# A graph network's last stage: the last node chunk in two parts, and up to six dense steps beside a gathered row

## The chip, the cores and the metric

One core of one Trainium2 chip runs the kernel. The metric is the device time of one execution in microseconds; 4676.03 us is the median of three runs of the kernel before (4673.82 to 4677.75). In the text PE is TensorE, DVE is VectorE, ACT is ScalarE, POOL is GpSimd and SP is SyncE.

## What is computed

A graph of 6250 nodes (64 features) and 200000 edges, sorted by target node. The first part is a two-layer edge-typed graph attention network with a residual and a layer norm. The second part, on which the change works, is this (`W`, `b` small, `pos`/`neg` the positive and negative part of the cosine):

```python
x  = layernorm(x + L0(x))              # two layers over the edges
Wh = x @ W + b
sim = cosine(Wh[src], Wh[dst])
base = edge_weight * softplus(deg[0] * edge_weight_n2 + deg[1]) * (src != dst)
prop = segment_sum(base * (c0 * relu(sim) - c1 * relu(-sim)) * Wh[dst], src)
out = layernorm(x + scale * (prop + c2 * Wh))
```

## The kernel before

The edges lie in 112 rows of 14 tiles of 128 edges. Because the targets are sorted, the targets of a row fall into a window of 80 nodes. Stages run one after another: a table of messages per node, `fast_path(0)`, a second table, `fast_path(1)` with the first 56 rows of layer 1, and then `last_rows` (L993), the only stage that the change touches. It does three things at once.

**The last 56 rows of layer 1.** For each row GpSimd issues 14 indirect gathers into `lrows` (L1158), which has four row buffers (`RB`), so a row's gather waits until the row four before it is used up. ACT scales the 14 tiles by the edge weights (L1351, in four parts, "wt"), DVE builds a one-hot matrix (L1411, "hot"), PE multiplies the two (L1248, "sum"), and DVE adds the result to the node sums `feat`, a window wide (L1422, "add", which also frees the buffer).

**The chunks of nodes.** Once all rows that reach a chunk of 7 node tiles (896 nodes) are added, the chunk can be finished: 19 steps over PE, DVE, ACT and SP (`STEPS`) turn the sums back, add residuals, apply the layer norm (`layer`, `centre`, `layer2`; L1428 to L1446), form `Wh` (`bias`, L1471), store it to memory, normalise it (`unit`, L1480), turn it in two halves (`HALF`), copy strips of it (ACT, L1378, "win") and load strips of `Wh` (SP, "load"). `needs` is the number of rows that must be added first: 0, 0, 0, 9, 25, 41 and 56 for the seven chunks.

**The dense part.** `fast_path` has stored for each of 56 groups of edges a dense matrix of edge weights, 128 targets by all 6272 nodes. A dense step, a "unit" (b, p), takes one pair of groups p (28 of them) and one block b of 448 nodes (14 of them), so there are 392. PE makes cosines (L1219), ACT takes their positive part (L1342), DVE blends (L1395) and multiplies with the loaded block of the matrix (`weigh`, L1147), and PE adds the product (L1238) into a PSUM bank. In a row DVE does every multiplication; after the rows GpSimd does every second one. Cosines have two buffers; the product runs three units behind. Consecutive units of one block are a visit. At its end DVE copies or adds the bank to `out_t` (`kept`, L1397, here called a block sum; L1403 is the add); the last visit of each block is copied by ACT instead (L1339) and goes into the output. A chunk's units can only run when the chunk is finished: chunk c opens its own two blocks for all pairs so far, and for older blocks the pairs that it adds (`READY`: 3, 7, 11, 15, 19, 23, 28 pairs). Before the rows end one bank is used, then two alternate.

**The order** is written out by a planner (L1022) that all engines follow. Between the parts of a row it calls `some`, which puts up to two chunk steps and one unit in the plan: four times around the scaling, and `OWN - 4` times between a row's sum and its add.

```python
OWN = 5
for c in range(NCH):
    first_of.append(len(units))
    for b in range(2 * c + 2):
        ps = range(before[c] if b < 2 * c else 0, READY[c])
...
if todo_u < first_of[done // len(STEPS)]:
    plan.append(("unit", todo_u))
```

A unit is planned only when its chunk is complete, so a chunk whose rows are not yet there leaves the calls empty. The plan has 256 units in the rows (4 and 2 in rows 0 and 1, five in most; none in rows 25 and 41, one in rows 26 and 42, four in rows 24 and 40) and 136 behind them. The last visits of blocks 2c and 2c+1 are followed by output chunk c: PE turns it (L1309, L1311), DVE adds and normalises (`result`, L1458 to L1469), SP stores. There are seven.

Of the kernel before, what the change touches and what calls it, by code (L numbers as in the profile page):

```python
# [14 lines left out]
P = 128  # L15
F = 64
# [44 lines left out]
READY = [4 * (c + 1) - 1 for c in range(NCH - 1)] + [PAIRS]  # L61
# [12 lines left out]
def build(nc, A, out):  # L74
    ctx = ExitStack()
    with ctx:
# [916 lines left out]
        def last_rows():  # L993

            CB, NA, LAG = 4, 4, 3
            OWN = 5
# [12 lines left out]
            first_visit = len(visits) - 2 * NCH  # L1009
# [58 lines left out]
            with ExitStack() as s4, scope() as s12, nc.Block() as block:  # L1068
# [19 lines left out]
                stage_u = both[:, :].rearrange("p (c a f) -> p c a f", c=CH, a=2)  # L1088
# [22 lines left out]
                s_whg = [ls(f"whg{c}") for c in range(NCH)]  # L1111
# [3 lines left out]
                HALF = ((0, 4), (4, CH - 4))  # L1115
# [4 lines left out]
                def tiles(c):  # L1120
                    return slice(c * CH, (c + 1) * CH)

# [41 lines left out]
                def _(sp):  # L1164
# [10 lines left out]
                    for event in plan:  # L1175
# [5 lines left out]
                        elif event[0] == "fin":  # L1181
                            c, step = event[1:]
                            if step == "store":
# [5 lines left out]
                                sp.dma_start(wh_rows.ap()[c * CH * P:(c + 1) * CH * P, :].rearrange("(i p) f -> p i f", p=P), skip[:, tiles(c), :]).then_inc(s_tab, 16)  # L1189
# [12 lines left out]
                    sp.wait_ge(s_whg[NCH - 1], 16 * len(groups_of(NCH - 1)))  # L1202
# [4 lines left out]
                def _(pe):  # L1207
                    def cosines(u):
                        b, p = units[u]
                        for c in range(NCH):  # L1210
# [11 lines left out]
                    def product(u):  # L1222
# [3 lines left out]
                        for c in range(NCH):  # L1226
# [24 lines left out]
                    def turn(c, half, src, width, s):  # L1251
                        lo, n = HALF[half]
# [4 lines left out]
                    def x_tile(c, j):  # L1257
                        return x_sb[:, c * CH + j, :]
# [4 lines left out]
                    for event in plan:  # L1263
# [8 lines left out]
                        elif event[0] == "fin":  # L1272
                            c, step = event[1:]
                            if step == "back":
                                if needs[c]:
                                    pe.wait_ge(s_add, needs[c])
                                if c:
                                    pe.wait_ge(s_uk, 2 * c)
                                for j in range(CH):
                                    last = pe.transpose(ps_h[:, j * F:(j + 1) * F], feat[:, (c * CH + j) * P:(c * CH + j + 1) * P], ident[0:F, 0:F])  # L1280
# [4 lines left out]
                            elif step == "xt1":  # L1285
                                pe.wait_ge(s_xk, 2 * c + 1)
                                turn(c, 1, x_tile, F, s_xt)
                            elif step == "wh":
                                pe.wait_ge(s_xk, 2 * c + 2)
                                for j in range(CH):  # L1290
# [5 lines left out]
                            elif step == "ut1":  # L1296
                                pe.wait_ge(s_uk, 2 * c + 1)
                                turn(c, 1, u_tile, P, s_ut)
                        elif event[0] == "out" and event[2] == "turn":
                            c = event[1]  # L1300
                            emptied(pe, first_visit + 2 * c + 1)
                            if c < NCH - 1:
                                pe.wait_ge(s_o_free, first_visit)
                            pe.wait_ge(s_uk, 2 * NCH)
                            if c:
                                pe.wait_ge(s_ovar, c)
                            for j in range(CH):
                                if c < NCH - 1:
# [9 lines left out]
                def _(act):  # L1318
# [3 lines left out]
                    def unit_kept(c, half):  # L1322
                        lo, n = HALF[half]
                        at = (c * CH + lo) * P
# [4 lines left out]
                    for event in plan:  # L1329
# [24 lines left out]
                        elif event[0] == "fin":  # L1354
                            c, step = event[1:]
                            if step == "std":
                                act.wait_ge(s_var, c + 1)
                                act.activation(mom[:, 2, tiles(c)], mom[:, 1, tiles(c)], ACT.Sqrt).then_inc(s_std, 1)
                            elif step in ("xk0", "xk1"):
                                half = int(step[2])  # L1360
                                lo, n = HALF[half]
                                act.wait_ge(s_xt, 2 * c + half + 1)
                                act.activation(xt[:, lo * P:(lo + n) * P], ps_h[0:F, 0:n * P], ACT.Copy).then_inc(s_xk, 1)
                            elif step == "nrm":
                                act.wait_ge(s_sq, c + 1)
                                act.activation(mom[:, 3, tiles(c)], mom[:, 0, tiles(c)], ACT.Sqrt).then_inc(s_nrm, 1)
                            elif step in ("uk0", "uk1"):
                                half = int(step[2])
                                act.wait_ge(s_ut, 2 * c + half + 1)
# [3 lines left out]
                            elif step == "win":  # L1373
                                act.wait_ge(s_uk, 2 * c + 2)
# [11 lines left out]
                def _(dve):  # L1386
# [10 lines left out]
                    def kept(k):  # L1397
                        b, lo, hi = visits[k]
                        part = out_t[:, b * SB:(b + 1) * SB]
                        dve.wait_ge(s_prod, hi + 1)  # L1400
                        if again[k]:
                            dve.wait_ge(s_o_free, again[k][-1] + 1)
                            dve.tensor_tensor(part, part, bank(k)[:, 0:SB], ALU.add).then_inc(s_o_free, 1)  # L1403
                        else:
                            dve.tensor_copy(part, bank(k)[:, 0:SB]).then_inc(s_o_free, 1)
# [8 lines left out]
                    def add_sums(r):  # L1414
# [6 lines left out]
                        part = feat[:, bass.ds(window, WIN)]  # L1421
                        dve.tensor_tensor(part, part, ps_sum[0:F, 0:WIN], ALU.add).then_inc(s_add, 1)  # L1422

                    def spread(ap, n):
                        return ap.rearrange("p (i o) -> p i o", o=1).to_broadcast([P, CH, n])

                    def centre(i, s_done):
                        link(dve.tensor_reduce(mom[:, 0, i], t1[:, :, :], AX.X, ALU.add))  # L1428
                        link(dve.tensor_scalar(mom[:, 0, i], mom[:, 0, i], 1.0 / F, None, ALU.mult))
                        link(dve.tensor_tensor(t1[:, :, :], t1[:, :, :], spread(mom[:, 0, i], F), ALU.subtract))  # L1430
                        link(dve.tensor_tensor(t2[:, :, :], t1[:, :, :], t1[:, :, :], ALU.mult))
                        link(dve.tensor_reduce(mom[:, 1, i], t2[:, :, :], AX.X, ALU.add))
                        dve.tensor_scalar(mom[:, 1, i], mom[:, 1, i], 1.0 / F, EPS_LN, ALU.mult, ALU.add).then_inc(s_done, 1)

                    def layer(c):
                        i = tiles(c)
                        dve.wait_ge(s_back, c + 1)
                        link(dve.tensor_tensor(t1[:, :, :], ps_h[:, 0:CH * F].rearrange("p (c f) -> p c f", f=F), skip[:, i, :], ALU.add))
                        link(dve.tensor_tensor(t1[:, :, :], t1[:, :, :], x_sb[:, i, :], ALU.add))
                        centre(i, s_var)  # L1440

                    def layer2(c):
                        i = tiles(c)
                        dve.wait_ge(s_std, c + 1)
                        link(dve.reciprocal(mom[:, 3, i], mom[:, 2, i]))
                        dve.tensor_tensor(x_sb[:, i, :], t1[:, :, :], spread(mom[:, 3, i], F), ALU.mult).then_inc(s_xn, 1)  # L1446
# [9 lines left out]
                    def result(c):  # L1456
# [4 lines left out]
                        centre(i, s_ovar)  # L1461

                    def result2(c):
# [5 lines left out]
                        dve.tensor_tensor(ready[c % 2], t1[:, :, :], spread(mom[:, 1, i], F), ALU.mult).then_inc(s_ready, 1)  # L1469

                    def bias(c):  # L1471
                        i = tiles(c)
                        dve.wait_ge(s_wh, c + 1)
                        dve.tensor_tensor(skip[:, i, :], ps_h[:, 0:CH * F].rearrange("p (c f) -> p c f", f=F),
                                          b2[:, :].rearrange("p (o f) -> p o f", o=1).to_broadcast([P, CH, F]), ALU.add).then_inc(s_skip, 1)
                        dve.wait_ge(s_skip, c + 1)
                        link(dve.tensor_tensor(t2[:, :, :], skip[:, i, :], skip[:, i, :], ALU.mult))
                        dve.tensor_reduce(mom[:, 0, i], t2[:, :, :], AX.X, ALU.add).then_inc(s_sq, 1)

                    def unit(c):  # L1480
                        i = tiles(c)
# [285 lines left out]
```

## Time and profile before

| | us |
|---|---|
| runs, median of 3 | 4676.03 (4673.82 to 4677.75) |
| the profiled execution, its own time | 4682.8 |
| its span in the profile | 4679.8 |
| PE busy | 3153.3 (67%) |
| DVE busy | 3124.3 (67%) |
| ACT busy | 1572.7 (34%) |
| GpSimd busy | 3240.7 (69%) |

The profile is one execution, a hardware trace of every instruction. The page groups it; the windows view cuts it into stretches with each engine's busy time, the granted clock of TensorE (1.00 is 2.4 GHz, 0.50 is 1.2 GHz) and the DMA share; the timeline lists instructions in order, with the idle time before each on its engine and what ended it in square brackets. A wait for several things is put down to the one that came last. `last_rows` begins at about 3297 us and ends at 4671 us.

### The profile page before, as it was taken

To read this page: it belongs to the slowest core of one execution; us is meant where nothing else is said; L and a number is where in the kernel's file an instruction comes from. 1 tells how busy PE (TensorE), PEld (TensorE's weight loads), DVE (VectorE), ACT (ScalarE), POOL (GpSimd) and SP (SyncE) were. 2 spreads that over 40 slices of the span, in tenths; PEclk is the share of its full clock that TensorE was granted. 3 is DMA by queue.
4 is the path that set the end of the run, shared out by engine and by line. 5 is a ranking of instruction groups with operands and counts; after the bars stand their busy time and mean duration, and the time that the engine had idled before them with its cause. 6 is when DMAs were issued, how large, how long until landed. Compare 5 with 4: busy or idle time off the path is not lost. (4 is left out here: it accounts for less than half of the span.)

```text
span 4679.8 us, 63684 instructions
## 1 busy us (share of the span) xinstructions
PE 3153.3 (67%) x16225; PEld 1888.5 (40%) x16225; DVE 3124.3 (67%) x5180; ACT 1572.7 (34%) x3260; POOL 3240.7 (69%) x3224
## 2 busy tenths in 40 slices
PE   4676777677777677676555656555476767677888
PEld 3344554445455444454344434444222222322232
DVE  6776777667777777774655555554477767677787
ACT  3422323232322322233421221221344545444434
POOL 0577777777777777774477777776666777776556
PEclk7888888888888888887777877787588989889999
DMA  3333323233333333332322222222355545555566
GB/s 63 122 93 91 97 90 101 83 96 93 97 94 90 98 91 95 92 97 80 111 72 67 77 71 68 76 72 66 110 155 144 165 125 165 137 152 155 169 176 193
DMA packets 355301, 502.07 MB, mean 107 GB/s; under 512 B 93127, under 2 KB 214984, under 8 KB 354809
## 3 DMA queue, kind: packets, MB, share of 16 engines
q1 hardware_dynamic: 251689, 394.52, 26.0%
q0 software_dynamic: 100352, 102.96, 10.7%
q8 instruction: 124, 2.03, 0.2%
q14 instruction: 240, 1.97, 0.1%
q10 hardware_dynamic: 2896, 0.59, 0.1%
HBM read 290.63 MB, written 207.16 MB: 106 GB/s over the span
## 5 line engine op out<-in xcount | busy, mean ns | idle before, releaser
L835 POOL DMA_INDIRECT frows<-messages,fidx x2352 | 2290.5, 974 | 828.5 <-issue 669.1
L915 PE MATMUL fps_b<-hot_key,hot_lo 128*128 128x343 f32 x3136 | 1237.8, 501 | 415.3 <-PEq L71 408.4
L974 DVE TENSOR_TENSOR strip<-strip,fps_b 128x343 f32 x1568 | 787.7, 502 | 552.9 <-DVEq L71 540.8
L850 ACT ACTIVATE turned<-fps_t 128x512 f32<-128x512 f32 (+1 forms) x754 | 431.9, 573 | 1755.6 <-ACTq L71 1749.2
L905 PE MATMUL fps_sum<-hot,frows 128*64 128x80 f32 x4704 | 555.1, 303 | 600.1 <-PEq L71 600.1
L1158 POOL DMA_INDIRECT lrows<-messages,lidx x784 | 744.9, 950 | 295.4 <-issue 223.2
L915 PEld LDWEIGHTS fps_b<-hot_key,hot_lo 128*128 128x128 f32 x3136 | 540.7, 206 | 742.4 <-issue 695.9
L905 PEld LDWEIGHTS fps_sum<-hot,frows 128*64 128x64 f32 x4704 | 526.3, 196 | 688.8 <-issue 688.8
L944 DVE TENSOR_SCALAR hot_key<-iota_f,edge 128x343 f32<-128x343 f32 x1574 | 751.5, 478 | 0.2
L1342 ACT ACTIVATE pos<-l_c,coeff 128x896 f32<-128x896 f32 x392 | 394.7, 1007 | 580.7 <-PE l_c L1219 579.8
L1219 PE MATMUL l_c<-unit_t,unit_g 64*128 64x448 f32 x1568 | 434.7, 632 | 132.7 <-DVE acc L1147 70.6
L899 PE MATMUL fps_t<-ident,strip 128*128 128x128 f32 x2842 | 474.4, 291 | 33.2 <-PEq L71 33.2
L899 PEld LDWEIGHTS fps_t<-ident,strip 128*128 128x128 f32 x2842 | 379.6, 151 | 234.0 <-issue 107.1
L841 ACT ACTIVATE strip<-zcol 128x512 f32<-128x512 f32 (+2 forms) x758 | 470.9, 621 | 0.0
L1395 DVE SCALAR_TENSOR_TENSOR l_c<-l_c,coeff,pos 128x896 f32<-128x896 f32 x256 | 295.1, 1153 | 253.4 <-ACT pos L1342 252.5
L988 DVE TENSOR_TENSOR frows<-frows,edge 128x896 f32<-128x896 f32 x168 | 182.6, 1087 | 291.0 <-DMA frows<-messages,fidx 288.5
L938 DVE TENSOR_TENSOR hot_lo<-fps_iota,edge 128x896 f32<-128x896 f32 x226 | 246.0, 1089 | 140.6 <-issue 139.6
L1238 PE MATMUL l_o<-acc,wh_g 128*64 128x448 f32 x1008 | 266.8, 610 | 71.4 <-DVE sums_t L1403 53.8
L1219 PEld LDWEIGHTS l_c<-unit_t,unit_g 64*128 64x128 f32 x1568 | 128.0, 198 | 391.6 <-DVE acc L1147 126.6
L938 DVE TENSOR_TENSOR hot<-fps_iota,edge 128x1120 f32<-128x1120 f32 x168 | 220.7, 1314 | 0.0
L1147 DVE TENSOR_TENSOR acc<-l_c,edge 128x896 f32<-128x896 f32 x192 | 209.5, 1091 | 6.6
L1351 ACT ACTIVATE lrows<-lrows,edge 128x64 f32<-128x64 f32 x784 | 208.6, 336 | 15.1 <-DMA lrows<-messages,lidx 15.0
(191 smaller groups left out, 1936.5 us busy)
## 6 DMA issues: line engine op xcount, KB each, us to landing
adj<-turned SPq DMA_DIRECT2D x696, 256.0 KB
edge<-adj SPq DMA_DIRECT2D x294, 448.0 KB
adj_x<-adj SPq DMA_DIRECT2D x98, 448.0 KB
frows<-messages,fidx POOLq DMA_INDIRECT x2352, 2.4
messages<-msg SPq DMA_DIRECT2D x14, 1120.0 KB, 4.6
lrows<-messages,lidx POOLq DMA_INDIRECT x784
adj<-turned SPq DMA_DIRECT2D x58, 64.0 KB
wh_g<-wh_rows SPq DMA_DIRECT2D x56, 32.0 KB, 1.8
```

Source lines behind the costliest of these rows:

```text
L835: pool.indirect_dma_start(rows[:, q, k, :], None, tab_l[l].ap(), bass.IndirectOffsetOnAxis(ap=idx[:, q, k:k + 1], axis=0)).then_inc(s_got[ ...
L841: return act.activation(part, zcol[:, 0:1].rearrange("p (a b) -> p a b", a=1).to_broadcast([P, n, STRIP]), ACT.Copy)
L850: act.activation(turned[j][:, 0:(b - a) * P], ps_t[j][:, 0:(b - a) * P], ACT.Copy).then_inc(s_t_free, 1)
L899: last = pe.transpose(ps_t[side(k, piece)][:, n * P:(n + 1) * P], strip[k][:, hi, :], ident[:, :])
L905: last = pe.matmul(ps_sum[0:F, 0:WIN], rows[:, u % RB, k, :], hot[:, u % 2, k, :], start=(k == 0), stop=(k == JT - 1))
L915: pe.matmul(ps_b[n % KB][:, 0:NT * TWIN], hot_lo[:, s % 2, k, :], hot_key[:, n % KB, :], start=True, stop=True).then_inc(s_b, 1)
L938: return dve.tensor_tensor(out_ap, ps_iota[:, 0:width].rearrange("p (o c) -> p o c", o=1).to_broadcast([P, n, width]), per_edge(array, at, ...
L944: dve.tensor_scalar(hot_key[:, n % KB, :], iota_f[:, :], edge[:, A_KEY, bass.ds(at, 1)], edge[:, A_BASE, bass.ds(at, 1)], ALU.is_equal, AL ...
L974: dve.tensor_tensor(part, part, ps_b[n % KB][:, 0:NT * TWIN].rearrange("p (h w) -> p h w", w=TWIN), ALU.add).then_inc(v, 1)
L1158: pool.indirect_dma_start(rows[:, q, k, :], None, tab_l[1].ap(), bass.IndirectOffsetOnAxis(ap=idx[:, q, k:k + 1], axis=0)).then_inc(s_got[ ...
L1219: last = pe.matmul(ps_c[u % 2][:, h, 0:SB], unit_g[h * F:(h + 1) * F, p, :], unit_t[h * F:(h + 1) * F, b * SB:(b + 1) * SB], start=True, s ...
L1342: act.activation(pos[:, u % 2, :, :], ps_c[u % 2][:, :, 0:SB], ACT.Relu, scale=coeff[:, 4:5]).then_inc(s_pos, 1)
```

## The change

The chunks of the dense part no longer have one size. Their bounds are a table of tiles, `BOUNDS`, in which the last chunk of 7 tiles is divided into one of 4 (512 nodes) and one of 3 (384). `SIZE`, `BLOCKS` (448-node blocks that are complete), `READY`, `needs` and the semaphore counts come from it: `READY` is 3, 7, 11, 15, 19, 23, 25, 28, and `needs` is 0, 0, 0, 9, 25, 41, 51, 56. A chunk of at most four tiles has one part instead of two halves and 15 steps. `OWN` is 6, so two units may stand between a row's sum and its add. Block 12 is complete with the new seventh chunk and block 13 with the last, and the first 12 blocks are visited once more: 69 visits instead of 56, 392 units as before. The final turn of the last output chunk now also reads `out_t`, whose last block is cleared beforehand. The operations of a chunk work on its own number of tiles.

```diff
-            OWN = 5
+            OWN = 6
+            BOUNDS = (0, 7, 14, 21, 28, 35, 42, 46, 49)
+            NC = len(BOUNDS) - 1
+            SIZE = [hi - lo for lo, hi in zip(BOUNDS, BOUNDS[1:])]
+            BLOCKS = [P * hi // SB for hi in BOUNDS[1:]]
+            READY = [(P * hi - 352) // 224 + 1 for hi in BOUNDS[1:-1]] + [PAIRS]
+            HALVES = [((0, 4), (4, n - 4)) if n > 4 else ((0, n),) for n in SIZE]
+            HB = [sum(len(k) for k in HALVES[:c]) for c in range(NC + 1)]
...
-            for c in range(NCH):
+            upto = [0] * NSB
+            for c in range(NC):
                 first_of.append(len(units))
-                for b in range(2 * c + 2):
-                    ps = range(before[c] if b < 2 * c else 0, READY[c])
+                for b in range(BLOCKS[c]):
+                    if BLOCKS[c] % 2 and c < NC - 2 and b < BLOCKS[c - 1]:
+                        continue
+                    ps = range(upto[b], READY[c])
+                    upto[b] = READY[c]
                     visits.append((b, len(units), len(units) + len(ps) - 1))
                     units += [(b, p) for p in ps]
...
-            needs = [max(0, 16 * (c + 1) + 1 - first_row) if c < NCH - 1 else n_rows for c in range(NCH)]
+            needs = [max(0, -(-P * BOUNDS[c + 1] // SLOPE_ROW) + 1 - first_row) if c < NC - 1 else n_rows for c in range(NC)]
...
-            chain = [(c, step) for c in range(NCH) for step in STEPS]
+            chain = [(c, step) for c in range(NC) for step in STEPS if SIZE[c] > 4 or step not in ("xt1", "xk1", "ut1", "uk1")]
+            chunks_done = [sum(1 for k in range(n) if chain[k][1] == "load") for n in range(len(chain) + 1)]
...
-                    if todo_u < first_of[done // len(STEPS)]:
+                    if todo_u < first_of[chunks_done[done]]:
...
                             for j in range(CH):
-                                if c < NCH - 1:
-                                    pe.matmul(ps_h[:, j * F:(j + 1) * F], out_t[:, (c * CH + j) * P:(c * CH + j + 1) * P], eye2[:, :], start=True, stop=False)
+                                pe.matmul(ps_h[:, j * F:(j + 1) * F], out_t[:, (c * CH + j) * P:(c * CH + j + 1) * P], eye2[:, :], start=True, stop=False)
                                 at = c % 4 * CH * P + j * P
-                                last = pe.matmul(ps_h[:, j * F:(j + 1) * F], rest_t[:, at:at + P], eye2[:, :], start=(c == NCH - 1), stop=True)
+                                last = pe.matmul(ps_h[:, j * F:(j + 1) * F], rest_t[:, at:at + P], eye2[:, :], start=False, stop=True)
...
-                    def centre(i, s_done):
-                        link(dve.tensor_reduce(mom[:, 0, i], t1[:, :, :], AX.X, ALU.add))
+                    def centre(i, m, s_done):
+                        a, b = t1[:, 0:m, :], t2[:, 0:m, :]
+                        link(dve.tensor_reduce(mom[:, 0, i], a, AX.X, ALU.add))
...
                     def layer2(c):
-                        i = tiles(c)
+                        i, m = part(c), SIZE[c]
+                        if c == NC - 1:
+                            dve.memset(out_t[:, (NSB - 1) * SB:NSB * SB], 0.0).then_inc(s_zero, 1)
```

## Rows read from the trace of the kernel before

**Rows 1.** The page of the kernel before, its first line.
```profile
span 4679.8 us, 63684 instructions
```
**Rows 2.** Windows of the last stage: stretch, us, busy per engine, clock, DMA share, GB/s.
```profile
3512.70:3568.40 55.70, 38.95 (x179) 16.46 (x179) 33.90 (x44) 23.06 (x58) 32.23 (x33) 0.79 0.42 112
3568.40:3791.80 223.40, 165.01 (x936) 63.23 (x936) 175.34 (x177) 117.11 (x281) 168.01 (x178) 0.96 0.61 168
3791.80:3830.90 39.10, 17.88 (x107) 12.56 (x107) 13.38 (x22) 13.36 (x44) 29.66 (x32) 0.65 0.22 51
3830.90:4044.50 213.60, 157.78 (x884) 59.94 (x884) 165.85 (x168) 109.64 (x259) 161.49 (x172) 0.96 0.60 167
4044.50:4097.00 52.50, 27.88 (x159) 17.88 (x159) 23.33 (x33) 21.04 (x67) 39.70 (x43) 0.67 0.32 80
4097.00:4324.80 227.80, 163.67 (x876) 61.92 (x876) 165.48 (x167) 108.11 (x253) 157.23 (x167) 0.92 0.58 156
4324.80:4374.70 49.90, 34.79 (x137) 11.71 (x139) 30.97 (x41) 17.31 (x28) 14.30 (x6) 0.76 0.34 94
...
4659.00:4671.30 12.30, 4.70 (x28) 2.17 (x26) 7.97 (x13) 0.75 (x2) 2.86 (x1) 0.82 0.00 0
```
**Rows 3.** The gathers of L1158: durations, GpSimd's idle before them, and who waits.
```profile
L1158 POOL DMA_INDIRECT lrows<-messages,lidx x784: 938/945/1561, 3296.7 to 4303.9; - x196
...
  issue: 223.2, 724
  POOLq L71: 72.2, 60
...
  ACT lrows L1351: 15.0, 4
```
**Rows 4.** Timeline: start, us, instruction. First gathers of rows 14, 41, 55; add of 55.
```profile
3568.55 0.94 POOL L1158 DMA_INDIRECT lrows<-messages,lidx  x1 [11.93 <-POOLq L71]
...
4042.82 0.94 POOL L1158 DMA_INDIRECT lrows<-messages,lidx  x1 [0.30 <-issue]
...
4287.62 0.94 POOL L1158 DMA_INDIRECT lrows<-messages,lidx  x1 [0.30 <-issue]
...
4324.82 0.22 DVE L1422 TENSOR_TENSOR sums_t<-sums_t,l_sum 64x80 f32 x1
```
**Rows 5.** Timeline of DVE, one row of five steps, from add to add.
```profile
3967.90 0.22 DVE L1422 TENSOR_TENSOR sums_t<-sums_t,l_sum 64x80 f32 x1
...
3980.89 1.16 DVE L1395 SCALAR_TENSOR_TENSOR l_c<-l_c,coeff,pos 128x896 f32<-128x896 f32 x1 [2.70 <-ACT pos L1342]
...
3983.09 0.22 DVE L1422 TENSOR_TENSOR sums_t<-sums_t,l_sum 64x80 f32 x1
```
**Rows 6.** Groups by line and form, 3200 to 4680 us: count, busy us, mean ns, idle before.
```profile
L1395 DVE SCALAR_TENSOR_TENSOR l_c<-l_c,coeff,pos 128x896 f32<-128x896 f32 x256 | 295.1, 1153 | 253.4 <-ACT pos L1342 252.5 <-issue 0.9
...
L1147 DVE TENSOR_TENSOR con_x<-l_c,adj_x 128x896 f32<-128x896 f32 x64 | 69.8, 1091 | 2.2
...
L1403 DVE TENSOR_TENSOR sums_t<-sums_t,l_o 128x448 f32<-128x448 f32 x30 | 18.2, 608 | 0.0
...
L1430 DVE TENSOR_TENSOR t<-t,mom 128x448 f32<-128x448 f32 x14 | 8.8, 625 | 2.1
```
**Rows 7.** Timeline behind the rows, PE and DVE.
```profile
4353.49 1.12 PE L1254 MATMUL l_h<-ident,both 128*128 128x128 f32 x4 [7.17 <-DVE both L1485]
...
4375.49 1.02 PE L1219 MATMUL l_c<-unit_t,unit_g 64*128 64x448 f32 x4
...
4377.35 1.02 PE L1219 MATMUL l_c<-unit_t,unit_g 64*128 64x448 f32 x4
...
4418.07 2.49 DVE L1458 SCALAR_TENSOR_TENSOR t<-skip,coeff,x_sb 128x448 f32<-128x448 f32 x1
...
4445.42 2.50 DVE L1458 SCALAR_TENSOR_TENSOR t<-skip,coeff,x_sb 128x448 f32<-128x448 f32 x1
...
4663.76 1.77 PE L1311 MATMUL l_h<-eye,lrows 128*128 128x64 f32 x14 [0.64 <-ACT lrows L1339]
```

More of the change, by code:

```diff
@@ L1110, in last_rows @@
                     ls(n) for n in ("back", "var", "std", "xn", "xt", "xk", "wh", "skip", "sq", "nrm", "u", "ut", "uk", "win"))
-                s_whg = [ls(f"whg{c}") for c in range(NCH)]
+                s_whg = [ls(f"whg{c}") for c in range(NC)]
                 s_oback, s_ovar, s_ostd, s_ready, s_gain = (ls(n) for n in ("oback", "ovar", "ostd", "ready", "gain"))
@@ L1121, in tiles, with part @@
                     return slice(c * CH, (c + 1) * CH)
+                def part(c):
+                    return slice(BOUNDS[c], BOUNDS[c + 1])
                 def weighed(eng, u):
@@ L1209, in cosines @@
                         b, p = units[u]
-                        for c in range(NCH):
+                        for c in range(NC):
                             if u == first_of[c]:
@@ L1225, in product @@
                         _, lo, hi = visits[k]
-                        for c in range(NCH):
+                        for c in range(NC):
                             if u == first_of[c]:
@@ L1277, in _ @@
                                 if c:
-                                    pe.wait_ge(s_uk, 2 * c)
-                                for j in range(CH):
-                                    last = pe.transpose(ps_h[:, j * F:(j + 1) * F], feat[:, (c * CH + j) * P:(c * CH + j + 1) * P], ident[0:F, 0:F])
+                                    pe.wait_ge(s_uk, HB[c])
+                                for j in range(SIZE[c]):
+                                    at = (BOUNDS[c] + j) * P
+                                    last = pe.transpose(ps_h[:, j * F:(j + 1) * F], feat[:, at:at + P], ident[0:F, 0:F])
                                 last.then_inc(s_back, 1)
@@ L1365, in _ @@
                                 act.wait_ge(s_sq, c + 1)
-                                act.activation(mom[:, 3, tiles(c)], mom[:, 0, tiles(c)], ACT.Sqrt).then_inc(s_nrm, 1)
+                                act.activation(mom[:, 3, part(c)], mom[:, 0, part(c)], ACT.Sqrt).then_inc(s_nrm, 1)
                             elif step in ("uk0", "uk1"):
                                 half = int(step[2])
-                                act.wait_ge(s_ut, 2 * c + half + 1)
+                                act.wait_ge(s_ut, HB[c] + half + 1)
                                 if c == 0 and half == 0:
@@ L1402, in kept @@
                             dve.wait_ge(s_o_free, again[k][-1] + 1)
-                            dve.tensor_tensor(part, part, bank(k)[:, 0:SB], ALU.add).then_inc(s_o_free, 1)
+                            dve.tensor_tensor(total, total, bank(k)[:, 0:SB], ALU.add).then_inc(s_o_free, 1)
                         else:
-                            dve.tensor_copy(part, bank(k)[:, 0:SB]).then_inc(s_o_free, 1)
+                            dve.tensor_copy(total, bank(k)[:, 0:SB]).then_inc(s_o_free, 1)
                     def weights(r):
@@ L1420, in add_sums @@
                             dve.wait_ge(s_add, r)
[L1421 to L1425, printed above, removed]
-                    def centre(i, s_done):
-                        link(dve.tensor_reduce(mom[:, 0, i], t1[:, :, :], AX.X, ALU.add))
+                        sums = feat[:, bass.ds(window, WIN)]
@@ new lines, in add_sums, with spread, turned @@
+                        dve.tensor_tensor(sums, sums, ps_sum[0:F, 0:WIN], ALU.add).then_inc(s_add, 1)
+                    def spread(ap, m):
+                        return ap.rearrange("p (i o) -> p i o", o=1).to_broadcast([P, m, F])
+                    def turned(m):
+                        return ps_h[:, 0:m * F].rearrange("p (c f) -> p c f", f=F)
+                    def centre(i, m, s_done):
+                        a, b = t1[:, 0:m, :], t2[:, 0:m, :]
+                        link(dve.tensor_reduce(mom[:, 0, i], a, AX.X, ALU.add))
@@ L1439, in layer @@
-                        link(dve.tensor_tensor(t1[:, :, :], t1[:, :, :], x_sb[:, i, :], ALU.add))
-                        centre(i, s_var)
+                        link(dve.tensor_tensor(t1[:, 0:m, :], turned(m), skip[:, i, :], ALU.add))
+                        link(dve.tensor_tensor(t1[:, 0:m, :], t1[:, 0:m, :], x_sb[:, i, :], ALU.add))
+                        centre(i, m, s_var)
                     def layer2(c):
-                        i = tiles(c)
+                        i, m = part(c), SIZE[c]
```

72 lines of the change are left out of this document (34 added, 38 removed).

## The prediction, made before the changed kernel ran

> **What bounds the kernel now.** The page gives the span [rows 1], and the change touches only the last stage, `last_rows`, so I cut that stage with the windows view [rows 2]. Busy shares decide nothing there (no engine is above 80% in the rows); what matters is who waits for whom. Three regimes show.
>
> Rows 0 to 55 are paced by two loops tied together. GpSimd issues 14 gathers a row: 945 ns plus the issue gap 223.2/724 = 0.31 us [rows 3], and the gathers of rows 41 and 55 start at 4042.82 and 4287.62 [rows 4]: 244.80/14 = **17.49 us a row**. A gather may start only when the row four before it is added, and where that is late GpSimd stands: 72.2 us in all, 32 of them before the stage, 11.93 at row 14 [rows 3, 4]. The other loop is PE, ACT and DVE. A row with five dense steps and no block sum takes 3983.09 - 3967.90 = 15.19 us from one add to the next, 2.70 of them DVE waiting behind PE's row sum [rows 5]. A step costs DVE 1153 + 1091 ns [rows 6], 2.24 us, so a row has 15.19 - 5 x 2.24 = 4.0 us of its own. Rows 11 to 24 (69 steps) took 223.4 us: 14 x 4.0 + 69 x 2.24 = 210.6, and 12.8 left for nine block sums that DVE drains there; rows 27 to 39 leave 16.0 for ten [rows 2]. I take 1.5 us a sum: 0.6 on DVE, and by the code PE's next block waits until its one bank is drained. Five-step rows, 16 us, are faster than the gather, so the gather sets the pace late in the stage.
>
> After row 55 nothing is gathered. Two steps' first matmuls lie 4377.35 - 4375.49 = 1.86 us apart [rows 7], PE without a gap: **PE-bound at 1.855**. Each output chunk adds 27.35 - 10 x 1.855 = 8.8 us [rows 7]. Between them the last chunk's chain: in 49.9 us only 12 steps run [rows 2] (22.3 us worth), **27.6 us lost**.
>
> **The change part by part.** Working both plans out from the code: 392 steps either way. Before, 256 lie in rows and 136 behind them. After, 271 in rows and 121 behind; rows 2 to 19, 27 to 37 and 43 to 55 hold six, but rows 21 to 25 and 39 to 41 hold none, because steps of a chunk wait until its nodes are summed (rows 25, 41, now also 51) and six a row use them up sooner. So the sixth step does not spread the work, it packs it.
>
> *Six a row.* 4.0 + 6 x 2.24 = 17.4 us, with about 0.9 sum a row 18.7: slower than 17.49. The 120 steps before row 25's chunk end at row 20, not 24, saving four row overheads: 3791.8 - 4 x 4.0 = 3775.8 (before, it is compute that paces up to here, GpSimd standing until row 14). Row 19 was added 13.0 before: 3762.8. Gather 23 cannot start sooner, gather 24 at 3780.3, gather 25 at **3797.8**. Before, gather 25 started 16 rows before gather 41: 4042.82 - 279.8 = 3763. The gather is 35 us late and cannot catch up, since it has no slack; five empty rows only let compute wait for it.
>
> *Rows 25 and 26.* ACT scales a row in order, before the chunk's square root, so it waits for the data. From gather start to add takes 4324.82 - 4287.62 = 37.2 [rows 4], less the 15.2 of a row: data 22 us after the start, 3819.8. The two rows with the chunk chain took 39.1 us with one step [rows 2], now three: 43.6, less 5 for the eight short DVE steps that run while ACT waits: row 26 ends at 3858.4. The same sum for rows 41 and 42 of before gives 4042.8 + 22 + 39.1 - 5 = 4098.9; it was 4097.0 [rows 2].
>
> *Rows 27 to 55.* Rows 27 to 37: 11 x 4.0 + 66 x 2.24 + 10 x 1.5 = 206.8, to 4065.2. Gather 41 starts at 3797.8 + 279.8 = 4077.6, row 42 ends at 4077.6 + 22 + 43.6 - 5 = 4138.2. Rows 43 to 55: 13 x 4.0 + 78 x 2.24 + 12 x 1.5 = 244.7, and the new four-tile chain in rows 51 to 53. A seven-tile chain in full rows cost, in rows 9 and 10, 55.7 - 8 - 22.4 - 2 x 1.5 = 22.3 [rows 2]; by tiles alone 12.7. I take 14, nearer the low end, as it also lacks both second halves. On SP it puts one more store, then four table loads, ahead of block loads; those run four ahead. Row 55 is added at 4396.9, against 4324.8: **+72**. By the gather alone it would be 4077.6 + 244.8 + 37.2 = 4359.7: the late rows are compute-bound now.
>
> *The tail.* Fifteen steps fewer: -27.8. The last chain has three tiles, six window copies on ACT instead of ten and 54 steps beside it, not 20, but only two chain steps go between two steps. It stood longest on DVE, 7.17 us at once [rows 7]. A DVE operation has a size-free part: 625 ns at 448 wide and 1091 at 896 [rows 6] give 159 ns, so 192 wide costs 358, which I keep, not 268. Bounds of its loss: 27.6 x 3/7 = 11.8, and 27.6; I take 16.6, **-11**. Thirteen block sums more, 608 ns each [rows 6], come in the tail, where two banks alternate. Two steps take PE 3.71 us and DVE 2 x 1153 + 1091 = 3.4 us, since GpSimd multiplies every other one, so part of each is hidden: from 0 to 13 x 1.5 = 19.5, I take **+3**. The clear of the last block (no wider than a 448-wide operation) hides while the square root is awaited; uncovered it costs 0.6. The last output turn has 28 matmuls, not 14, which took 1.77 [rows 7]: +1.8, on the path. Tail: **-34**.
>
> **Rivals.**
> *A, faster: the extra steps fall into idle time.* For it: DVE is busy under 80% of the row windows, and ACT waits 15.0 us for gathered rows [rows 3], time that is free. If rows with six steps stay under 17.49 us, row 55 stays at 4324.8 and the tail gives 34: **4642**. It decides where a six-step row with its sums is under the gather's time. Against: of the 15.19 us DVE waits 2.70, for PE's row sum, and a sixth step behind that sum waits no less, so it adds its 2.24.
> *B, no change: only the early rows are late.* Gather 25 is 35 us late as worked out, but the last 13 rows keep up with it (block sums or the chain hide): row 55 at 4359.7, +34.9 - 34 = +1: **4677**.
> *C, slower still.* The chain in rows costs the full 22.3, the last chain gains nothing, the sums in the tail cost 19.5: +8 + 11 + 16.5 more: **4750**. For it: DVE's L1458 takes 2.49 us [rows 7] where others of its width take 0.625 [rows 6], with GpSimd multiplying beside it; if the thirteen sums met that, 1.87 us each, it would be 24 instead of 19.5. Against: a sum reads one PSUM bank and one SBUF tile, as L1395 does at 1153 ns, while L1458 reads two SBUF tiles; but the 608 ns were measured while GpSimd only gathered. The Trainium skill (SBUF — State Buffer, "SBUF: two separate sides") says that DVE operations with two SBUF inputs and GpSimd's operations exclude each other from a shared port pair. By that rule the sums are spared; the stretched L1458 agrees with it.
>
> **How the numbers follow.** The summed case 0.64, A 0.12, B 0.16, C 0.08. I trust the lateness of the gather most, since before every row up to 14 the same four-row rule shows as GpSimd standing; I trust the chain costs least. The main case itself spans 4694 to 4734 (chain in rows 12.7 to 22.3, last chain 11.8 to 27.6, sums 0 to 19.5, not all at one end). The range reaches down to B and below, 4668, and up towards C, 4738, leaving A and part of C out. Faster 0.12, same 0.16, slower 0.72.
>
> **What would show it.** Right: gather 25 starts near 3798 and gather 55 near 4322, with GpSimd standing some 35 us more than 72.2 in all before row 25; adds in rows 27 to 37 about 18.7 us apart and in rows 21 to 24 at the gather's pace; row 55 added near 4397; some 312 us from there to the end, against 346. Wrong: six-step rows under 17.5 us, row 55 below 4360, a chain of waits in the tail that names block sums, or a gain in the tail far from 34.

## The result, and the profile after

The changed kernel takes **4710.82 us** (median of 4 runs, 4704.14 to 4720.15) against 4676.89 (4, 4673.82 to 4679.33): ratio 1.0075, 95% interval 1.0063 to 1.0087. The forecast was 4714. The execution profiled took 4720.15 us, 9.3 above the median, with this page in place of [rows 1]:

```profile
span 4718.5 us, 63770 instructions
```

First the three quantities that the prediction tied together: a row with six steps, the gather of row 25, and the end of the rows. Timeline of DVE and GpSimd (start us, duration, instruction, idle before):

```profile
3748.32 0.22 DVE L1433 TENSOR_TENSOR sums_t<-sums_t,l_sum 64x80 f32 x1
3765.70 0.22 DVE L1433 TENSOR_TENSOR sums_t<-sums_t,l_sum 64x80 f32 x1
...
3794.06 0.23 DVE L1433 TENSOR_TENSOR sums_t<-sums_t,l_sum 64x80 f32 x1 [8.81 <-PE l_sum L1260]
3811.39 0.23 DVE L1433 TENSOR_TENSOR sums_t<-sums_t,l_sum 64x80 f32 x1 [15.87 <-PE l_sum L1260]
...
3858.48 0.22 DVE L1433 TENSOR_TENSOR sums_t<-sums_t,l_sum 64x80 f32 x1
```

```profile
3802.41 0.94 POOL L1170 DMA_INDIRECT lrows<-messages,lidx  x1 [0.30 <-issue]
...
4328.54 0.94 POOL L1170 DMA_INDIRECT lrows<-messages,lidx  x1 [0.54 <-issue]
```

The first pair are the adds of rows 18 and 19: 17.38 us apart, six steps and no block sum. Rows 23 and 24 have no steps left, and DVE stands for their sums: there the gather paces. It starts row 25 at 3802.4 and row 55 at 4328.5, 40.9 us behind [rows 4]. What GpSimd waited for in its gathers:

```profile
L1170 POOL DMA_INDIRECT lrows<-messages,lidx x784: 938/944/1819, 3297.4 to 4344.8; - x196
...
  issue: 223.8, 721
  POOLq L70: 112.1, 63
```

The issue gaps are those of [rows 3]; the wait for a free row buffer grew from 72.2 to 112.1 us. Windows cut at the same events as [rows 2] (us, busy per engine, clock, DMA share, GB/s): rows 11 to 24, 25 and 26, 27 to 37, 41 and 42, 43 to 55, then the last chain:

```profile
3593.60:3811.40 217.80, 152.91 (x848) 62.91 (x848) 151.06 (x154) 105.61 (x267) 152.15 (x162) 0.88 0.54 148
3811.40:3858.50 47.10, 20.99 (x119) 12.49 (x119) 17.57 (x27) 16.17 (x49) 35.82 (x38) 0.67 0.26 60
3858.50:4065.90 207.40, 158.32 (x840) 56.92 (x840) 164.93 (x165) 104.14 (x233) 156.80 (x167) 0.95 0.63 173
4091.60:4138.60 47.00, 20.56 (x119) 12.19 (x119) 17.52 (x26) 16.10 (x49) 35.72 (x38) 0.67 0.26 60
4138.60:4398.90 260.30, 196.56 (x1004) 71.94 (x1004) 199.32 (x210) 123.94 (x277) 156.59 (x166) 0.91 0.59 160
4398.90:4430.00 31.10, 23.60 (x91) 7.25 (x91) 21.15 (x37) 11.98 (x19) 11.43 (x4) 0.83 0.44 123
```

Row 55 is added at 4398.94, 74.1 us later than before, and the last instruction stands 310.4 us behind it, where it stood 346.3. In the tail, the timeline of PE and DVE: the longest stall of the last chain, an output's first operation, and the last turn.

```profile
4415.78 0.33 PE L1266 MATMUL l_h<-ident,both 128*128 128x128 f32 x1 [3.53 <-DVE both L1503]
...
4537.38 2.50 DVE L1475 SCALAR_TENSOR_TENSOR t<-skip,coeff,x_sb 128x448 f32<-128x448 f32 x1
...
4557.30 2.50 DVE L1475 SCALAR_TENSOR_TENSOR t<-skip,coeff,x_sb 128x448 f32<-128x448 f32 x1
...
4700.39 0.43 PE L1320 MATMUL l_h<-eye,sums_t 128*128 128x64 f32 x2 [0.64 <-ACT lrows L1350]
```

The stall is 3.53 us for 7.17 [rows 7]. Outputs are 19.93 us apart (the last two pairs 20.4), six steps and 8.8 us, the same surcharge as before. By the count of steps and the times all seemed explained; the experiments showed that it was not.

### The profile page after: what moved, and what is told of

The parts are those of the page before. It is cut to its first block and busy times, and to the rows that moved or that the text cites. A ratio compares the mean times of both kernels' runs of the same rounds, so it can differ in the third digit from the quotient of the medians.

```text
span 4718.5 us, 63770 instructions
## 1 busy us (share of the span) xinstructions
PE 3175.1 (67%) x16239; PEld 1896.0 (40%) x16239; DVE 3140.2 (67%) x5218; ACT 1572.2 (33%) x3262; POOL 3214.7 (68%) x3216
## 5 line engine op out<-in xcount | busy, mean ns | idle before, releaser
L1406 DVE SCALAR_TENSOR_TENSOR l_c<-l_c,coeff,pos 128x896 f32<-128x896 f32 x271 | 312.5, 1153 | 238.0 <-ACT pos L1353 237.9
L1250 PE MATMUL l_o<-acc,wh_g 128*64 128x448 f32 x1096 | 296.5, 622 | 65.3 <-DVE sums_t L1414 48.9
L1159 POOL TENSOR_TENSOR acc<-acc,edge 128x896 f32<-128x896 f32 x60 | 168.7, 2812 | 183.3 <-DVE acc L1406 173.9
L1159 DVE TENSOR_TENSOR acc<-l_c,edge 128x896 f32<-128x896 f32 x204 | 222.7, 1092 | 7.0
```

## The experiments

Every run is given as its median and its ratio to the kernel before, run beside it on the same chip (4676.8 to 4679.6 us in the four groups of runs). The intervals reach 0.1 to 0.14 per cent to either side.

### Split and sixth step apart

**E1**, the changed kernel with `OWN = 5`.
```diff
-            OWN = 6
+            OWN = 5
```

> The changed kernel with OWN = 5: the last chunk divided, five steps a row as before. My theory (the sixth step costs, the split is about neutral): gather 25 starts where it did before (3762), row 55 is added 3 to 8 us later than before because of the four-tile chain in rows 51 to 53 (its 14 us stand against the slack of five-step rows under the gather), and the tail behind it gives 136 steps as before with a chain 11 us cheaper, 2 to 3 us for the block sums and 1.8 for the last turn: 4673 to 4679 us, no change. Rival (the split itself is what costs, through its thirteen sums and its second chain): over 4690.

Measured 4657.46 us (4653.48 to 4661.86), 0.9960 [0.9947, 0.9974]: a gain of 19 us that no theory had. Counted from the stage's first gather, row 55 is added 1.1 us later than before; the whole gain lies in the tail, 324.4 us for 346.3.

**E2**, the kernel before with `OWN = 6`.
```diff
-            OWN = 5
+            OWN = 6
```

> The kernel before with OWN = 6: no split, up to six steps a row. My theory: gathers as late as in the changed kernel (gather 25 near 3802), row 55 added near 4384 (the changed kernel's 4398.9 less its chain of 15 us in the rows), 15 steps fewer behind it at 1.855 us: 59 - 28 = +31, 4704 to 4712 us. Rival (six steps gain by themselves and the split spoils it): below 4677.

Measured 4687.71 us, 1.0018 [1.0008, 1.0028]: dearer, as the theory has the sign, but 16 us below its range.

**E3**, the changed kernel, sixth step up to row 42 only, and **E4**, from row 43 only.
```diff
-                some(OWN - len(PARTS), r)
+                some((6 if r < 43 else 5) - len(PARTS), r)
```

> The changed kernel with six steps only in rows 0 to 42 and five behind. My theory: the late gather is caused here, so gather 25 still starts near 3802 and gather 55 near 4328; rows 43 to 55 then keep up with the gather, row 55 is added near 4368, 258 steps lie in the rows: 4368 + 335 against 4671, +30 us, 4700 to 4712. Rival (the late rows, compute-bound at six, carry the loss): 4680 or less.

Measured 4696.43 us (4689.3 to 4698.97), 1.0037 [1.0023, 1.0050]: 4 us below the theory's range and 16 above the rival's. Row 55 is added at 4374.0 (4368 expected), and the tail is 313.7 instead of 335.
```diff
-                some(OWN - len(PARTS), r)
+                some((6 if r >= 43 else 5) - len(PARTS), r)
```

> The changed kernel with five steps in rows 0 to 42 and six only behind. My theory: gather 25 and row 42 as before (3762, 4097), rows 43 to 55 take 260 us as in the changed kernel, row 55 added near 4357, 269 steps in the rows, tail 315 us: +1, 4673 to 4683 us, so the late six cost nothing and gain nothing. Rival (late rows carry the loss): 4700 or more.

Measured 4677.45 us, 1.0001 [0.9992, 1.0010]. So the early sixth steps carry the cost, the late ones next to none. But E1 and E2 don't add: the split is worth -0.40 per cent with five steps and +0.57 with six.

### The gather's lateness by itself

A fifth row buffer in the last stage lets a gather start when the row five before it is added, not four. `t1` and `t2` move into spare memory to make room, and GpSimd's loop is written out; the steps and their order stay.
```diff
+LRB = 5
...
-                rows = sb("lrows", [P, RB, JT, F], F32, s4)
+                rows = sb("lrows", [P, LRB, JT, F], F32, s4)
-                t1 = sb("t1", [P, CH, F], F32, s4)
-                t2 = sb("t2", [P, CH, F], F32, s4)
+                t1 = spare_a[:, 6 * SB:6 * SB + CH * F].rearrange("p (i f) -> p i f", f=F)
+                t2 = spare_e[:, 6 * SB:6 * SB + CH * F].rearrange("p (i f) -> p i f", f=F)
```
**E5**, in the changed kernel:

> The changed kernel with five row buffers in the last stage instead of four (two small tiles moved into free space, GpSimd's loop written out). My theory (a gather waits for the add four rows before, and that makes it late): with five it waits for the add five rows before, so gather 25 starts one row earlier, near 3784 instead of 3802, row 26 ends near 3841, row 55 near 4381: 17 us less than the changed kernel, 4690 to 4697. Rival (the lateness is the compute of six-step rows alone, the buffers don't matter): as the changed kernel, 4706 to 4714.

Measured 4695.51 us, 1.0035 [1.0021, 1.0049]. **E6**, in the kernel before:

> The kernel before with five row buffers. My theory: GpSimd stands some 9 us instead of 24 after the stage has begun, gathers of rows 15 on start about 15 us earlier, compute stays ahead to row 40 as it was and from there is no longer held by the gather: row 55 added 10 to 14 us earlier, 4662 to 4667. Rival (the late rows are bound by compute already): 4673 to 4680, no change.

Measured 4663.88 us, 0.9974 [0.9965, 0.9983]. Both lie in the theory's range. Counted from the stage's first gather, the gather of row 25 starts 18.0 us earlier in E5 than in the changed kernel and row 55 is added 16.9 earlier; in E6 it is 20.9 and 15.2 against the kernel before. So in both kernels the rows follow the gather's start. It isn't the loop written out that helps: the gathers of 14 rows (41 to 54) take 245.2 us in both runs, 244.8 in the kernel before. But the buffer doesn't undo the change either: with five buffers the change costs 0.61 per cent, with four 0.75, and the difference lies inside the intervals. E5's gathers, with the wait for a row buffer down from 112.1 to 93.1 us:

```profile
L1171 POOL DMA_INDIRECT lrows<-messages,lidx x784: 938/944/1816, 3294.7 to 4322.9; - x196
...
  POOLq L71: 93.1, 60
```

### Why E1, E2 and E3 have shorter tails

From the add of row 55 to the last instruction the traces have, in us, beside what the terms of the prediction make of it:

```
                     tail    by the terms   GpSimd's steps   outputs stand at
before               346.3   (given)        odd              odd steps
changed              310.4   312.3          even             even
E4 six late          314.9   316.0          even             even
E1 split, five       324.4   340.1          odd              even
E2 whole, six        301.6   318.5          even             odd
E3 six early         313.7   336.4          odd              even
```

After the rows GpSimd multiplies every other step, counted from the first one left (`(u - alone) % 2 == 1`). `alone` is 256 before and in E1, 271 in the changed kernel and E2, 258 in E3, 269 in E4. By the plans the outputs (but for the last) come right behind steps 289, 299, ... with the whole chunk and 334, 340, ... with the split one. Where both parities agree the tail is the long one, where they don't it is 16 to 23 us shorter than worked out. (E3 has the most: against E1 another 4.4 us in the steps beside the last chain and 1.9 in the last output, which the parity doesn't account for.) The timeline shows what an output meets. Kernel before, an output's first and last operation on DVE, and GpSimd's products:

```profile
4418.07 2.49 DVE L1458 SCALAR_TENSOR_TENSOR t<-skip,coeff,x_sb 128x448 f32<-128x448 f32 x1
4420.71 0.68 DVE L1460 SCALAR_TENSOR_TENSOR t<-l_h,gain,t 128x448 f32<-128x448 f32 x1
...
4428.68 2.17 DVE L1469 TENSOR_TENSOR both<-t,mom 128x448 f32<-128x448 f32 x1
```

```profile
4417.35 2.73 POOL L1147 TENSOR_TENSOR acc<-acc,edge 128x896 f32<-128x896 f32 x1 [0.97 <-DMA edge<-adj]
4427.50 2.86 POOL L1147 TENSOR_TENSOR con_x<-con_x,adj_x 128x896 f32<-128x896 f32 x1 [7.42 <-DVE con_x L1395]
```

GpSimd's first product ends at 4417.35 + 2.73 = 4420.08 and L1458 at 4420.56, 0.48 later; the second ends at 4430.36 and L1469 at 4430.85, 0.49 later. The next experiments turn the parity and nothing else (where 121 steps are left, GpSimd has 61 products instead of 60).
```diff
-            on_pool = [u for u in range(alone, len(units)) if (u - alone) % 2 == 1]
+            on_pool = [u for u in range(alone, len(units)) if (u - alone) % 2 == 0]
```
**E7**, in the kernel before:

> The whole chunk, five steps a row, but after the rows GpSimd multiplies the other parity of steps: those at an even distance from the first of them instead of those at an odd one. The same work for every engine (68 of 136 products on GpSimd either way). Theory (parity of the outputs): an output part whose first blend (2.50 us) and last product (2.16 us), both with two inputs in SBUF, run beside a GpSimd product costs VectorE 2.1 us more than one that runs clear of it (1.45 and 1.12 us in the kernel split with five steps); seven outputs turn from the first sort to the second, so 346 us after the last row become 331 to 334, and the time 4661 to 4665 us. Rival (the shorter tails of the runs with another number of steps have to do with the split or with where the rows end): nothing changes, 4674 to 4681 us.

Measured 4667.58 us (4661.01 to 4671.63), 0.9977 [0.9967, 0.9986]. It lies between the two ranges, 3 us above the theory's and 6 below the rival's, and its interval leaves out 1. Its tail is 336.2, 10.1 shorter: its outputs come 24.75 us apart (twice 25.4) instead of 27.35, which is 14 us with the last one, but the steps beside the last chain take 4 us longer. The same places in its timeline, DVE, then GpSimd:

```profile
4410.65 1.45 DVE L1458 SCALAR_TENSOR_TENSOR t<-skip,coeff,x_sb 128x448 f32<-128x448 f32 x1
4412.50 0.68 DVE L1460 SCALAR_TENSOR_TENSOR t<-l_h,gain,t 128x448 f32<-128x448 f32 x1 [0.40 <-PE l_h L1311]
...
4420.30 1.12 DVE L1469 TENSOR_TENSOR both<-t,mom 128x448 f32<-128x448 f32 x1
```

```profile
4408.82 2.79 POOL L1147 TENSOR_TENSOR acc<-acc,edge 128x896 f32<-128x896 f32 x1 [0.90 <-DMA edge<-adj]
4418.07 2.87 POOL L1147 TENSOR_TENSOR acc<-acc,edge 128x896 f32<-128x896 f32 x1 [6.45 <-DVE acc L1395]
```

GpSimd's product began earlier against the output here, ends at 4411.61, and L1458 ends at 4412.10, again 0.49 later; L1469 ends at 4421.42, 0.48 behind a product that ends at 4420.94. The instruction isn't slowed in proportion: it ends half a microsecond after GpSimd is done, whenever it began. That holds in every trace: 181 operations of this width with two SBUF inputs began while a product was running, and all ended 0.48 or 0.49 us behind it. The 1346 blends into which PSUM goes (L1395) that began beside one took 1.14 or 1.15 us, as they do alone. The Trainium skill (SBUF — State Buffer, "SBUF: two separate sides") describes this as "an exclusive lock, not a bandwidth split", held for a whole instruction, between a DVE operation with two SBUF inputs and a GpSimd operation; these ends agree with it.

**E8**, the changed kernel turned:

> The changed kernel (split, up to six steps a row) with the other parity of GpSimd's steps after the rows. Theory (parity of the outputs): its outputs take 2.50 and 2.16 us in those two instructions as before's do, and turn to 1.45 and 1.12: 310 us after the last row become 295 to 299, and the time 4694 to 4699 us. Rival (parity is nothing): 4706 to 4715 us.

Measured 4703.72 us, 1.0041 [1.0027, 1.0055]: again between the two ranges, 5 us above the theory's and 2 below the rival's. Both operations went as expected (below), and the tail is 296.1 for 310.4, inside its range. Against the changed kernel's 1.0075 the turn gained 0.34 per cent, 16 us.

```profile
4537.62 1.46 DVE L1475 SCALAR_TENSOR_TENSOR t<-skip,coeff,x_sb 128x448 f32<-128x448 f32 x1
...
4547.28 1.11 DVE L1486 TENSOR_TENSOR both<-t,mom 128x448 f32<-128x448 f32 x1
```

**E9**, the split with five steps (E1), turned:

> The split with five steps a row, with the other parity of GpSimd's steps after the rows. Theory (parity): its outputs here turn the wrong way, to 2.50 and 2.16 us, and its 324 us after the last row become 336 to 340, so 4670 to 4677 us: within 0.2 per cent of the kernel before, as the prediction priced the split by itself. Rival (the split itself gains the 20 us): 4653 to 4662 us as without the turn.

Measured 4680.45 us, 1.0003 [0.9994, 1.0012]: the whole gain of E1 is gone, and some 3 us more than I had put on it. Its tail is 348.8, not 336 to 340, against E1's 324.4. Some 15 us of that are six outputs (19.9 to 20.5 apart, for 17.1 to 18.3); the last output goes the other way, 0.67 us in its first operation for 2.50 in E1, and gives some 3 us back. Another 8.9 come in the steps beside the last chain: the 24th of them begins 66.2 us behind the add of row 55 for 57.3. There the chain's own operations meet GpSimd's products. E9, DVE, then GpSimd:

```profile
4326.52 1.72 DVE L1463 TENSOR_TENSOR x_sb<-t,mom 128x192 f32<-128x192 f32 x1
...
4335.46 1.85 DVE L1494 TENSOR_TENSOR t<-skip 128x192 f32<-128x192 f32 x1
...
4341.04 2.04 DVE L1501 TENSOR_SCALAR mom<-mom 128x3 f32<-128x3 f32 x1
```

```profile
4325.94 2.08 POOL L1159 TENSOR_TENSOR acc<-acc,edge 128x896 f32<-128x896 f32 x1 [29.71 <-DVE acc L1406]
4334.23 2.86 POOL L1159 TENSOR_TENSOR acc<-acc,edge 128x896 f32<-128x896 f32 x1 [6.21 <-DVE acc L1406]
4340.21 2.85 POOL L1159 TENSOR_TENSOR acc<-acc,edge 128x896 f32<-128x896 f32 x1 [3.11 <-DVE acc L1406]
```

In E1 the three take 0.36, 0.36 and 0.98 us, 3.9 less together. Another 3.3 us are lost at the 15th step, where GpSimd waits 5.42 us and DVE 1.91 for blocks of the matrix to be loaded; why these come late there isn't shown.

**E11**, the whole chunk with six steps (E2), turned:

> The whole chunk with up to six steps a row, and GpSimd's parity after the rows turned. In the run of this kernel without the turn the outputs took 1.45 and 1.12 us in their two long instructions. Theory (parity): the turn makes them 2.50 and 2.16 us, each of six outputs comes 2.5 us later, and the time rises from 4688 to 4700 to 4708 us, where the prediction's steps had put six steps a row. Rival (six steps a row cost only the 10 us seen, for another reason): 4684 to 4692 us.

Measured 4710.35 us (4702.47 to 4713.33), 1.0063 [1.0049, 1.0077]: 2 us above the range, and where the expectation of E2 had been (4704 to 4712). Eight kernels now stand in a square (ratio to the kernel before):

```
outputs beside GpSimd's products    whole     split
five steps a row                    1         1.0003  (E9)
six steps a row                     1.0063    1.0075  (E11, changed kernel)

outputs clear of them               whole     split
five steps a row                    0.9977    0.9960  (E7, E1)
six steps a row                     1.0018    1.0041  (E2, E8)
```

Read at equal parity, the sixth step costs 0.63 and 0.72 per cent beside GpSimd and 0.41 and 0.81 clear of it; the split moves -0.17 to +0.23; the turn is worth 0.23 to 0.45 in all four. With the intervals of each entry, the sixth step is the one dear edit and the split by itself has no settled sign. Two things blur the square. "Clear of them" means that an output's two long operations meet the last 1 us of a product, not none. And the last output stands behind an odd step in all eight, so with the split it has the other parity than the six before it: between whole and split stand the 2 to 3 us of that one output, 0.04 to 0.07 per cent. E3 and E4 can be read again too: early sixth steps cost 0.77 per cent (E1 to E3, both clear) or 0.74 (E4 to the changed kernel, both beside); late ones +0.04 (E3 to E8) or -0.02 (E9 to E4). In E4's trace row 55 comes 30.6 us later than in E9's, counted from the stage's first gather, and the tail is 33.9 shorter.

### Do the gains add?

**E10**, the split with five steps (E1) and five row buffers:

> The split with five steps a row, GpSimd's parity as it came, and five row buffers in the last stage in place of four. Theory (gather pace bounds five-step rows, and the tail is another account): the two gains add, 4657 less the 13 that five buffers gave the kernel before: 4640 to 4648 us. Rival (rows of five steps have no room left once the split's chains stand in them): 4653 to 4660 us.

Measured 4659.55 us, 0.9955 [0.9941, 0.9969], against 0.9960 for E1: the rival. From the add of row 50 to that of row 55 the kernel before takes 4324.8 - 4236.4 = 88.4 us, some of it waiting for the gather; with five buffers (E6) 76.1. In E1 and E10 the new chain stands in rows 51 and 52, and both take 92.4. So with four buffers the chain adds 4.0 us, since it takes the place of a part of that wait; with five it adds 16.3. At row 50 E1, E6 and E10 all stand 936.8 us behind the stage's first gather, so these five rows are where the fifth buffer had its gain. Adds of rows 50 and 55, E10:

```profile
4232.93 0.22 DVE L1434 TENSOR_TENSOR sums_t<-sums_t,l_sum 64x80 f32 x1
...
4325.27 0.22 DVE L1434 TENSOR_TENSOR sums_t<-sums_t,l_sum 64x80 f32 x1
```

**E12**, the kernel before with five buffers and turned:

> The whole chunk, five steps a row, five row buffers, GpSimd's parity turned. Theory (the buffers gain among the rows, the turn gains after them): the two gains, 0.26 and 0.23 per cent, add: 4650 to 4659 us, as fast as the split with five steps a row. Rival (they share one wait): 4661 to 4668 us.

Measured 4652.73 us (4651.45 to 4654.6), 0.9946 [0.9932, 0.9959]: the two gains add, without the split, and this is the lowest median of all. Its interval overlaps E10's and E1's, so which of the three is best stays open; all three beat both kernels.

## Why the prediction was right, point by point

**The mechanism held.** A row of six steps was put at 17.4 us and took 17.38. Row 19 was added at 3765.7 (3762.8 in the prediction), the gather of row 25 began at 3802.4 (3797.8), row 26 ended at 3858.5 (3858.4), row 37 at 4065.9 (4065.2), the gather of row 41 at 4082.6 (4077.6), row 42 ended at 4138.6 (4138.2), row 55 at 4398.9 (4396.9). Row 26 hit to 0.1 us by two errors that cancel: the gather of row 25 began 4.6 later than worked out, and from there to the add of row 26 it took 56.1 us where the prediction's sum has 60.6; with rows 41 and 42 it is the same, 5.0 and 56.0 for 60.6. That the rows follow the gather's start is shown by E5, where the gather of row 25 18.0 us earlier brought row 55 16.9 earlier. That it is the early sixth steps which make it late is shown by E3 and E4: at equal parity they cost 0.74 to 0.77 per cent, 35 us net, row 55 being 41.6 to 44.4 us later and the tail 4.5 to 10.7 shorter. The gather of row 25 was worked out as 35 us late and was 40.15 late.

**The four-tile chain in rows** was put at 14, within 12.7 to 22.3. Row 51 took 29.9 us, 12.6 above a full row, and row 53 2.3 above: 14.8. Against E2, which has no such chain, rows 51 to 55 took 14.2 longer. That it costs this in rows with six steps says nothing of rows with five: there it cost 4.0 (E1), part of its time standing where the gather was waited for anyway, and 16.3 with five buffers (E10).

**The tail** was put at -34 and gave -35.9: 15 steps -27.8; the last chain lost 16.3 us instead of 27.6 (11 products, 20.4 us worth, before the twelfth begins 36.7 us behind the add of row 55), so -11 (predicted -11); the block sums +2 (predicted +3: six times, four steps with two sums among them take 7.76 us for 7.42); the last turn, 28 matmuls in 3.3 us for 1.77, +1.5 (predicted +1.8). The clear did not hide beside the square root, as the prediction has it. The root (ACT) was there at 4403.59, and the clear stood before the next step of the chain and held it back some 0.3 us, which is within the chain's 16.3:

```profile
4403.38 0.21 ACT L1369 ACTIVATE mom<-mom 128x3 f32<-128x3 f32 x1 [0.92 <-DVE mom L1448]
```

```profile
4404.48 0.43 DVE L1460 MEMSET sums_t<- 128x448 f32 x1
4404.82 0.12 DVE L1462 RECIPROCAL mom<-mom 128x3 f32<-128x3 f32 x1
```

**The total** is +33.9 by the medians, +37.4 by the two profiled executions (4720.15 less 4682.8), for +38. That it is this close is in part luck: see row 26 above, and the outputs below.

**Rival A** (extra steps in idle time) needed six-step rows that, with their sums, stay below the gather's time; they took 17.4 without a sum and 207.4/11 = 18.9 with sums in rows 27 to 37. **Rival B** (only the early rows are late) gave 4677 for the right account of the early rows and the wrong one for the late: row 55 was 39 us behind its 4359.7. It took the tail's 34 us without their price: late sixth steps are steps moved out of the tail, and E4, where against E9 row 55 comes 30.6 us later and the tail is 33.9 shorter, takes the time that E9 takes. **Rival C** had DVE's long L1458 in it and asked whether block sums would meet the same wait; they did not: the 12 adds in the tail (L1414) took 617 ns at most, with GpSimd multiplying beside them.

**What was missed.** The step "each output chunk adds 8.8 us" was carried over unchanged as if it were a property of the output. It is one of its place against GpSimd's products, worth 2.3 to 2.6 us an output in the four pairs of traces. Moving 15 steps (an odd number) turned the parity, as E2 shows by itself; dividing the chunk turned where the outputs stand, as E1 shows; the change does both, and the two cancel. The prediction says nothing of this, so here it was right by luck: with one of the two alone the same arithmetic misses by 16 to 20 us, as my expectations of E1 and E2 did.

## What to carry to other kernels

When a loop's pace hangs on buffers, ask of every edit whether it packs work ahead of the point where the slower, steady loop (here the gather) must start; time lost there wasn't won back here, while the same work moved late was only moved. A term that is read off a periodic stretch, "so much an output", holds only as long as the two engines meet in the same phase: check in the timeline what the partner engine does at that instant, and which edits change an index's parity. Take two edits apart at equal phase before giving either its price.

## What the runs showed that was not expected

A DVE operation with two SBUF inputs of 448 elements ended 0.48 to 0.49 us after the end of the GpSimd product it met, 181 times out of 181 in the fourteen traces, whatever its start; so it took 2.49 or 1.45 us, 2.17 or 1.12. Other widths end later or sooner: 0.22 us behind the product at 192 elements (four of four) and 0.95 at 896 (twelve of twelve). That is the operation's time alone (0.67 or 0.62, 0.36, 1.08) less 0.13 to 0.19, as if it ran only when GpSimd was done; the profile shows the wait as the instruction's own duration, not as idle time before it. It isn't only operations with two inputs: a tensor_scalar of 3 or 7 elements with one SBUF input, 0.17 us alone, took 0.98 to 2.04 and ended 0.02 or 0.03 us behind the product, thirteen times of thirteen. With no product beside it, the first operation of the last output took 0.67 us in the changed kernel and the last 0.62, so that even the better parity leaves 0.8 and 0.5 us an output:

```profile
4698.64 0.67 DVE L1475 SCALAR_TENSOR_TENSOR t<-skip,coeff,x_sb 128x448 f32<-128x448 f32 x1
```

One line, the parity of GpSimd's steps, is worth 0.23 per cent of the whole kernel, and five row buffers in place of four 0.26.
